# Probabilities times values in two 16-bit parts, two tiles at once, and a new schedule around it

## Time and profile before

| what | value |
|---|---|
| three runs, median (lowest to highest) | 429.23 us (428.6 to 437.26) |
| the profiled execution, its own time | 431.57 us |
| its span, first to last instruction | 429.3 us |
| mean granted TensorE clock | 0.946 of 2.4 GHz |
| busy: PE, DVE, ACT, POOL | 348.2, 302.6, 210.7, 237.0 us |
| scatter-adds L491, 64 of them | 102.9 us busy |
| product L1521, 16 tiles | 35.6 us busy |

### The profile page before, as it was taken

How to read it: one execution, slowest core, us unless ns; L and a number is a source line. 1 busy time by engine, 2 the same in 40 slices (tenths; PEclk the granted TensorE clock), 3 DMA queues, 4 the chain that set the end, 5 groups by cost and what they waited for, 6 DMA issues and landing times.

```text
span 429.3 us, 7070 instructions
## 1 busy us (share of the span) xinstructions
PE 348.2 (81%) x2108; PEld 273.3 (64%) x2108; DVE 302.6 (70%) x953; ACT 210.7 (49%) x540; POOL 237.0 (55%) x219
## 2 busy tenths in 40 slices
PE   0999668778798998669979999987278877987893
PEld 0984336647375877648847788765156766876773
DVE  4599975568646765235777586656679998899875
ACT  3755436252532534353334454432257678676871
POOL 3600085676757668676867788852156545764211
PEclk9999999896978999879998999999869999999999
DMA  8957935575658998766776778557700000000001
GB/s 271 361 176 247 329 99 126 117 178 117 148 99 198 243 279 209 186 134 135 197 171 124 167 164 187 91 61 166 252 2 0 26 1 27 26 24 27 2 25 50
DMA packets 33032, 58.41 MB, mean 136 GB/s; under 512 B 3723, under 2 KB 20451, under 8 KB 32611
## 3 DMA queue, kind: packets, MB, share of 16 engines
q1 hardware_dynamic: 20707, 39.08, 27.9%
q0 software_dynamic: 12288, 18.88, 24.7%
HBM read 40.22 MB, written 17.73 MB: 135 GB/s over the span
## 4 chain that ended last, share of the span: by engine, by line
PE 42%; DVE 27%; issue 11%; ACT 9%; DMA 6%; POOL 4%; DVEq 0%; POOLq 0%; ACTq 0%
PE two L1521 7%; PE two L1541 6%; PE two L1553 5%; DMA acc_d<-W,idxE 4%; PE two L1483 3%; DVE F L1263 3%; PE two L1360 3%; PE two L1409 2%; POOL ny L534 2%; PE two L1435 2%; PE two L1530 2%; PE two L1494 2%; ACT W L789 2%; ACT two L776 2%; DVE WoS L958 2%
## 5 line engine op out<-in xcount | busy, mean ns | idle before, releaser
L491 POOL DMA_INDIRECT acc_d<-W,idxE x64 | 102.9, 1608 | 51.3 <-DVE W L1081 36.0
L472 POOL DMA_INDIRECT W<-tok_d,idxE x56 | 57.6, 1029 | 48.2 <-DVE idxE L1039 31.4
L1117 DVE SCALAR_TENSOR_TENSOR W<-W,two 128x88 f32<-128x88 f32 x64 | 15.6, 244 | 59.9 <-ACT W L703 45.5
L687 ACT ACTIVATE W<-two 128x256 f32<-128x256 f32 x64 | 24.3, 380 | 45.8 <-PE two L1530 40.3
L1521 PE MATMUL two<-A,v 128*128 128x128 f32 x256 | 35.6, 298 | 10.3 <-issue 7.5
L1521 PEld LDWEIGHTS two<-A,v 128*128 128x128 f32 x256 | 34.2, 212 | 13.3 <-issue 12.7
L1667 PE MATMUL two<-W,A 128*128 128x257 f16 x256 | 30.1, 273 | 10.6 <-DVE F L1288 9.9
L1634 PE MATMUL two<-F,wfcT 128*128 128x256 f16 x256 | 32.8, 280 | 4.4 <-DVE A L1256 2.9
L1667 PEld LDWEIGHTS two<-W,A 128*128 128x128 f16 x256 | 23.9, 98 | 16.5 <-DVE F L1288 11.7
L1081 DVE TENSOR_SCALAR W<-two,W 128x256 f32<-128x256 f32 x56 | 26.8, 478 | 8.5 <-PE two L1553 5.1
L776 ACT ACTIVATE two<-two,gwv 128x512 f32<-128x512 f32 x32 | 21.3, 667 | 23.1 <-PE two L1634 23.1
(11 more groups left out here) (237 smaller groups left out, 882.8 us busy)
## 6 DMA issues: line engine op xcount, KB each, us to landing
W<-in_gu SPq DMA_DIRECT2D x20, 352.0 KB
acc_d<-F SPq DMA_DIRECT2D x2, 2176.0 KB, 14.2
F<-in_gu SPq DMA_DIRECT2D x12, 352.0 KB
W<-in_dn SPq DMA_DIRECT2D x20, 176.0 KB
tok_d<-xr SPq DMA_DIRECT2D x2, 1280.0 KB, 5.9
F<-in_dn SPq DMA_DIRECT2D x12, 176.0 KB
x<-in_q SPq DMA_DIRECT2D x4, 512.0 KB, 6.5
A<-in_Wo SPq DMA_DIRECT2D x1, 2048.0 KB, 12.5
```

The source lines that it names most:

```text
L472: pool.indirect_dma_start(out=xg[n % XR], out_offset=None, in_=tok_d[:, :], in_offset=bass.IndirectOffsetOnAxis(ap=idxE[:, n:n + 1], axis=0))\
L491: pool.indirect_dma_start(out=acc_d[n % 2][:, :], out_offset=bass.IndirectOffsetOnAxis(ap=idxE[:, n:n + 1], axis=0), in_=ysb[n % YS], in_o ...
L687: sc.activation(xgT[n % 2], bk_(2)[:, 0:D].rearrange("p (k n) -> p k n", k=KH), ACT.Copy)\
```

## The change

- The values are kept as a high and a low 16-bit part (`v_hi` by ACT, `v_lo` by DVE), and so are the transposed probabilities (`pT_hi`, `pT_lo`); the product is hi*hi + lo*hi + hi*lo.
- Two tiles of one batch share one product of 256 columns (`attend`), 24 instructions of 16 bits for two tiles. `ORDER` now takes two tiles of a batch in turn. ACT copies both results at once, and the projections of both follow in the next pair.
- A half of a transpose is copied by ACT and then subtracted by DVE, and only then may the bank be written again.
- All 16 tiles stand in the loop, from turn 17; behind it stands the last projection alone.
- Tables, slot products and the shared MLP get other turns, ACT takes 8 in place of 10 tiles of the last table pass, and DVE the other 8.
- Ahead of the loop, the transposes of the last two parts of the values follow the first token list, and DVE subtracts four parts; three in place of two of the head sums come behind the first list.

```diff
-START = 19
-LATE = 2
-BESIDE = (NT - LATE) * STEPS
-ACT_T = 10
+START = 17
+BESIDE = NT * STEPS
+ACT_T = 8
...
-DOWN_AT = {1: (0, 0), 2: (0, 1), 6: (1, 0), 7: (1, 1), 11: (2, 0), 12: (2, 1), 16: (3, 0), 17: (3, 1)}
-UP_AT = {3: 1, 8: 2, 13: 3}
-PRODUCT_AT = {4: 1, 9: 2, 14: 3}
+DOWN_AT = {1: (0, 0), 2: (0, 1), 5: (1, 0), 6: (1, 1), 9: (2, 0), 10: (2, 1), 13: (3, 0), 14: (3, 1)}
+UP_AT = {3: 1, 7: 2, 11: 3}
+PRODUCT_AT = {4: 1, 8: 2, 12: 3}
...
-HOT_AT = {2: (1, 0), 3: (1, 1), 4: (1, 2), 7: (2, 0), 8: (2, 1), 9: (2, 2), 12: (3, 0), 13: (3, 1), 14: (3, 2)}
-NUMBER_AT = {2: (1, 0), 3: (1, 1), 7: (2, 0), 8: (2, 1), 12: (3, 0), 13: (3, 1)}
-SLOTS_AT, SPREAD_AT, TURN_AT, TAKE_AT = {5: 1, 10: 2, 15: 3}, {6: 1, 11: 2, 16: 3}, {7: 1, 12: 2, 17: 3}, {8: 1, 13: 2, 18: 3}
+HOT_AT = {2: (1, 0), 3: (1, 1), 4: (1, 2), 7: (2, 0), 8: (2, 1), 9: (2, 2), 13: (3, 0), 14: (3, 1), 15: (3, 2)}
+NUMBER_AT = {2: (1, 0), 3: (1, 1), 7: (2, 0), 8: (2, 1), 13: (3, 0), 14: (3, 1)}
+SLOTS_AT, SPREAD_AT, TURN_AT, TAKE_AT = {6: 1, 12: 2, 17: 3}, {7: 1, 13: 2, 18: 3}, {8: 1, 14: 2, 19: 3}, {9: 1, 15: 2, 20: 3}
...
-ORDER = [p + NP * i for p in range(NP) for i in range(2)]
+ORDER = [NP * b + 2 * p + i for p in range(NP // 2) for b in range(BATCH) for i in range(2)]
+UW = 2 * P
...
 def beside(n):
...
-        v = sb("v", [P, NT, DH])
+        v_hi, v_lo = [sb(n, [P, NT, DH], F16) for n in ("v_hi", "v_lo")]
...
-        probT = [A[:, 2048 + 1024 * i:3072 + 1024 * i].rearrange("p (i j) -> p i j", i=8) for i in range(2)]
+        pT_hi, pT_lo = [A[:, 2048 + 1024 * i:3072 + 1024 * i].bitcast(F16).rearrange("p (i j) -> p i j", i=8) for i in range(2)]
...
-        oT = [F[:, 8128 + 128 * i:8256 + 128 * i] for i in range(2)]
+        oT = [F[:, 8128 + UW * i:8128 + UW * i + UW] for i in range(2)]
...
             def gated(p):
...
-                pool.wait_ge(s0_ready, 2 * p + 2)
+                pool.wait_ge(s0_ready, NT)
...
             def take_v(c):
...
-                sc.activation(v[:, 4 * c:4 * c + 4, :], bk_(c % 2).rearrange("p (t d) -> p t d", t=4), ACT.Copy)\
-                    .then_inc(v_ready, 1)
+                sc.activation(v_hi[:, 4 * c:4 * c + 4, :], bk_(c % 2).rearrange("p (t d) -> p t d", t=4), ACT.Copy)\
+                    .then_inc(v_hi_ready, 1)
...
             def number(g, t0, t1):
...
+            def high_probs(t, h):
+                sc.wait_ge(pT_ps, 2 * t + h + 1)
+                if t >= 2:
+                    sc.wait_ge(o_ps, t // 2)
+                sc.activation(pT_hi[:, 4 * h:4 * h + 4, P * (t % 2):P * (t % 2) + P], bk_(0).rearrange("p (i j) -> p i j", i=4), ACT.Copy)\
+                    .then_inc(pT_hi_ready, 1)
+            def take_oT(u):
+                sc.wait_ge(o_ps, u + 1)
+                if u >= 2:
+                    sc.wait_ge(wo_ps, 2 * u - 2)
+                sc.activation(oT[u % 2], bk_(1)[:, 0:UW], ACT.Copy).then_inc(oT_ready, 1)
             def attention_step(t, step):
...
-                    sc.wait_ge(pT_ps, 2 * t + 1)
-                    if t >= 2:
-                        sc.wait_ge(o_ps, t - 1)
-                    sc.activation(probT[t % 2][:, 0:4, :], bk_(0).rearrange("p (i j) -> p i j", i=4), ACT.Copy)\
-                        .then_inc(pT_act, 1)
-                elif step == 2 and t + 1 < NT:
-                    exps(t + 1)
-                elif step == 3:
-                    sc.wait_ge(o_ps, t + 1)
-                    if t >= 2:
-                        sc.wait_ge(wo_ps, t - 1)
-                    sc.activation(oT[t % 2], bk_(1)[:, 0:P], ACT.Copy).then_inc(oT_ready, 1)
+                    if t % 2 == 0 and t:
+                        take_oT(t // 2 - 1)
+                    high_probs(t, 0)
+                elif step == 2:
+                    high_probs(t, 1)
+                    if t + 1 < NT:
+                        exps(t + 1)
...
             def turn(n):
...
-            for t in range(NT - LATE, NT):
-                for step_ in range(STEPS):
-                    attention_step(t, step_)
+            take_oT(NT // 2 - 1)
...
             def gate(p):
...
+            def low_v(c):
+                ve.wait_ge(v_hi_ready, c + 1)
+                ve.tensor_tensor(v_lo[:, 4 * c:4 * c + 4, :], bk_(c % 2).rearrange("p (t d) -> p t d", t=4),
+                                 v_hi[:, 4 * c:4 * c + 4, :], ALU.subtract).then_inc(v_ready, 1)
...
             def take_projected(t):
-                ve.wait_ge(wo_ps, t + 1)
+                ve.wait_ge(wo_ps, t - t % 2 + 2)
...
-                then(ve.scalar_tensor_tensor(out=s0[:, u, :], in0=bk_(1)[:, 0:D], scalar=rinv[:, t:t + 1], in1=bo_b,
+                then(ve.scalar_tensor_tensor(out=s0[:, u, :], in0=bk_(1)[:, D * (1 - t % 2):D * (1 - t % 2) + D], scalar=rinv[:, t:t + 1], in1=bo_b,
...
+            def low_probs(t, h):
+                ve.wait_ge(pT_hi_ready, 2 * t + h + 1)
+                cols = slice(P * (t % 2), P * (t % 2) + P)
+                ve.tensor_tensor(pT_lo[:, 4 * h:4 * h + 4, cols], bk_(0).rearrange("p (i j) -> p i j", i=4),
+                                 pT_hi[:, 4 * h:4 * h + 4, cols], ALU.subtract).then_inc(pT_lo_ready, 1)
             def attention_step(t, step):
...
-                    if t:
-                        take_projected(t - 1)
-                elif step == 1 and t + 1 < NT:
-                    top(t + 1)
+                    low_probs(t, 0)
+                elif step == 1:
+                    if t + 1 < NT:
+                        top(t + 1)
...
-                    ve.wait_ge(pT_ps, 2 * t + 2)
-                    if t >= 2:
-                        ve.wait_ge(o_ps, t - 1)
-                    ve.tensor_copy(probT[t % 2][:, 4:8, :], bk_(0).rearrange("p (i j) -> p i j", i=4)).then_inc(pT_dve, 1)
+                    low_probs(t, 1)
+                    if t % 2 == 0 and t:
+                        take_projected(t - 2)
...
+                    if t % 2 == 0 and t:
+                        take_projected(t - 1)
...
             def flat_g(a):
...
+            low_v(0)
+            low_v(1)
...
-            head_sum(1)
...
-            head_sum(2)
-            head_sum(3)
+            low_v(2)
+            low_v(3)
+            for i in range(1, 4):
+                head_sum(i)
...
-            for t in range(NT - LATE, NT):
-                for step_ in range(STEPS):
-                    attention_step(t, step_)
+            take_projected(NT - 2)
...
-            turn_v(2)
-            turn_v(3)
...
+            turn_v(2)
+            turn_v(3)
...
             def turn_probs(t, h):
...
-                if h:
-                    pe.wait_ge(pT_act, t + 1)
-                elif t:
-                    pe.wait_ge(pT_dve, t)
+                if t or h:
+                    pe.wait_ge(pT_lo_ready, 2 * t + h)
+                else:
+                    pe.wait_ge(sy_ready, NT // 2)
...
             def project0(t):
-                pe.wait_ge(oT_ready, t + 1)
+                pe.wait_ge(oT_ready, t // 2 + 1)
...
-                pe.matmul(bk_(1)[:, 0:D], oT[t % 2], WoS[:, :], start=True, stop=True).then_inc(wo_ps, 1)
+                pe.matmul(bk_(1)[:, D * (1 - t % 2):D * (1 - t % 2) + D], oT[t // 2 % 2][:, P * (t % 2):P * (t % 2) + P], WoS[:, :],
+                          start=True, stop=True).then_inc(wo_ps, 1)
+            def attend(u):
+                pe.wait_ge(pT_lo_ready, 4 * u + 4)
+                if u:
+                    pe.wait_ge(s0_ready, 2 * u)
+                else:
+                    pe.wait_ge(idxE_ready, NG)
+                for i in range(8):
+                    k = (ORDER[2 * u] // NP) * NP + i
+                    for v, pT in ((v_hi, pT_hi), (v_hi, pT_lo), (v_lo, pT_hi)):
+                        ins = pe.matmul(bk_(1)[:, 0:UW], v[:, k, :], pT[:, i, :], start=(i == 0 and v is v_hi and pT is pT_hi),
+                                        stop=(i == 7 and v is v_lo))
+                ins.then_inc(o_ps, 1)
...
             def attention_step(t, step):
...
-                    if t:
+                elif step == 1:
+                    if t % 2 == 0 and t:
+                        project0(t - 2)
...
-                elif step == 1 and t + 1 < NT:
-                    score(t + 1)
+                    if t + 1 < NT:
+                        score(t + 1)
...
-                elif step == 3:
-                    pe.wait_ge(pT_act, t + 1)
-                    pe.wait_ge(pT_dve, t + 1)
-                    if t:
-                        pe.wait_ge(s0_ready, t)
-                    else:
-                        pe.wait_ge(idxE_ready, NG)
-                    for i in range(8):
-                        ins = pe.matmul(bk_(1)[:, 0:P], v[:, (ORDER[t] // NP) * NP + i, :], probT[t % 2][:, i, :], start=(i == 0),
-                                        stop=(i == 7))
-                    ins.then_inc(o_ps, 1)
+                elif t % 2:
+                    attend(t // 2)
...
             def turn(n):
...
-            for t in range(NT - LATE, NT):
```

(11 more changed lines are left out.)

## The result

The changed kernel takes 435.5 us (median of four runs) where the kernel before took 429.6 in the runs beside it: ratio 1.0148, 95% interval 1.0109 to 1.0186. It is 1.5% slower: clear of the interval, but less than the 2% that counts as a difference. The forecast was 425.2 us; the time lies just above the range's end at 435.0. The profiled execution has 436.2 us of its own and a span of 434.3, 5.0 more than the profiled one of before.

A forecast was written before the change was run, and what follows sets the result against it. PE (2.86 us per expert plus waits) and POOL (3.19 plus waits) were taken as nearly level bounds. +4.4 - 7.6 + 1.9 + 0 + 1.4 - 4.1 = -4.0 us gave a median of 425.2 us, range 418 to 435.

The forecast's parts named there:

- Ahead of the loop, +4.4: Before the first expert: DVE's extra head sum, low-part subtractions and wait for late transposes cost 4.4 us, bounds 3.2 to 5.5.
- Tables, -7.6: In the loop: later slot products spare PE's three 2.60 us waits and half the low clock, 7.6 us gained, bounds 0 to 14.2.
- the fourth rival: Ahead of the first experts: five us of PE work at half speed, +2.5 us, 427.7 us in all; chance 0.08.
- Product, split and two tiles, +1.9 and 0: Loop from turn 17: two more tiles' streaming costs 1.9 us if PE sets the pace; the split's order costs 0.
- My bounds, -6 to +20.8: Limits on the split's cost in the loop: pace falling to 3.27 us, or both halves' extra copy time bare 16 times.
- The sign of being wrong that I named: From expert 19: a pace over 3.5 us per expert with PE waiting for the subtraction; or a first expert not later.
- first rival: In the loop: DVE waits for ACT's high part, PE for DVE; +10.4 us, 435.6 us in all; chance 0.17.
- POOL's floor of 3.19: In the loop while gathers last: POOL unhindered starts a scatter-add, gather included, every 3.19 us, the floor of an expert.
- PE's level: In the loop: PE streams 2.86 us per expert, attention tiles included, plus waits, nearly level with POOL.
- End of the loop, +1.4: Turn 63: both last down products wait for a longer last product and longer copies, 1.4 us, none if POOL is behind.
- Behind the loop, -4.1: After the last scatter-add: without two leftover tiles the first total starts 3.1 to 5.1 us sooner, taken as 4.1.

The follow-up runs named there:

- e5: The kernel before with the later tables, slot products and shared MLP turns alone, old product, two tiles behind the loop: 424.0 us, ratio 0.983.
- e4: The changed kernel with the last pair's product behind PE's last two down products instead of ahead of them: 432.4 us, ratio 1.0086.
- e18: The changed kernel with only ACT's copy `gwv` put ahead of turn 34's steps, which moved nothing, so a repeat: 436.9 us, ratio 1.017.
- e9: The changed kernel, same steps and turns dealt so steps 0 and 1 share a turn, `gwv` copied earlier: 417.5 us, ratio 0.973.
- e10: The changed kernel, same steps and turns dealt so steps 2 and 3 share a turn, `gwv` copied earlier: 445.0 us, ratio 1.038.
- e1: The changed kernel without DVE's subtractions for the low parts of the probabilities, as many products: 427.9 us, ratio 1.0006.
- e2: The kernel before with the changed schedule alone: old product, later tables, all 16 tiles in the loop from turn 18: 435.1 us, ratio 1.015.
- e11: The kernel before with later tables and slot products, old product, steps 0 and 1 sharing a turn in 11 of 14 tiles: 416.8 us, ratio 0.971.
- e13: The kernel before with nothing of the change but steps 0 and 1 sharing a turn in 11 of 14 tiles: 423.2 us, ratio 0.980.
- e14: The changed kernel over the same 47 turns, steps 1 and 2 of every tile sharing a turn: 428.5 us, ratio 0.992.
- e15: The changed kernel over the same 47 turns, step 3 of each tile sharing a turn with step 0 of the next: 424.0 us, ratio 0.981.
- e16: The changed kernel's own deal, but steps 0 and 1 share a turn in the five tiles where 2 and 3 did: 431.8 us, ratio 1.001.
- e17: The changed kernel's own deal, DVE's sums over heads for layer 1 moved from turn 42 to turn 46: 427.6 us, ratio 0.992.

## Why the prediction was wrong

**Ahead of the loop, +4.4: right.** +3.8 at the first tanh (62.96 against 59.18), +3.9 at DVE's first expert, with no cover. The runs with these same instructions ahead of the loop have their first tanh from 62.5 to 65.1, so the agreement is no closer than 1 or 2 us.

**Tables, -7.6: right, its last tenths by luck.** From the first tanh to that of expert 19 it is 67.0 us in place of 74.7, 7.7 less, with 1.9 of loss inside that the sum did not have (below). With the tables alone (e5) it is 68.1, 6.6 less. The three waits of 2.60 are gone, the small ones ahead of `turn_h` that the forecast named are there twice (0.87 and 0.90 us), and the clock came back whole, where I took half: the product of table 1 follows PE's work without idle time (the chain, in order of time), and the clock of the stretch that had 0.50 is 1.00.

```profile
85.59 0.86 PE two L1438 x4
86.45 1.75 PE two L1454 x16
```
```profile
95.00:130.00 35.00, 31.65 (x167) 22.69 (x168) 29.45 (x117) 15.49 (x55) 26.71 (x20) 1.00 0.72 161
```

**The low clock ahead of the first experts** (the fourth rival) came too, inside that sum. Behind DVE's later start PE's clock was 0.73 from 65 to 71 us, where the kernel before had 1.00 from 62 to 67 (in e4 and e18, with the same instructions up to there, it was 0.50 from 65 to 71), and the first expert took longer (the shared product ahead of it, then its up products, beside those of the second expert):

```profile
65.00:71.00 6.00, 4.68 (x18) 3.61 (x19) 0.85 (x5) 2.47 (x7) 0.39 (x1) 0.73 0.16 47
```
```profile
67.28 1.63 PE two L1438 x4
68.92 0.43 PE two L1557 x2
69.34 1.17 PE two L1568 x4
70.52 0.21 PE two L1574
70.73 0.72 PE two L1580 x2
71.45 0.86 PE two L1438 x4
72.31 0.22 PE two L1557 x2
72.53 0.60 PE two L1568 x4
73.13 0.11 PE two L1574
73.24 0.43 PE two L1580 x2
```

So the rule of the Trainium skill that the prediction weighed ("TensorE: Matmul & The Clock Gate", "Part 1: The HAM clock gate": the clock is halved when the array has not been busy of late) held where the forecast took nothing for it. The five pieces take 4.16 us the first time and 2.22 the second, 1.9 us more; in the kernel before only the shared product was longer, 1.13 for 0.86. (The stretch of 303 to 313 that the forecast compares with has PE busy for 0.61 us, not 0.25.)

**Product, split and two tiles, +1.9 and 0: the step that failed.** The loop from expert 19 took 9.6 us more. The failed step is the sentence under the split, "yet PE finds the bank free where the steps fall in different turns. I take 0": it puts the order of the steps at nothing. I had counted how many steps a turn holds on average, 2.3 us for each, and never listed which steps share a turn. What the runs showed in its place: the order alone moves the loop from 141.9 us (e9) to 170.3 (e10), and the changed kernel's own deal stands at 159.2. My bounds, -6 to +20.8, did hold the size (the pace of the lower one, 3.27, is not half of the way from 3.40 to 3.19; that is 3.295, and about -5). The sign of being wrong that I named came: a pace of 3.62, over 3.5, with PE waiting for the subtraction.

The streaming was right where the clock was up: 24 instructions take 2.63 us on the chain (forecast 2.62). Two of the eight took 5.08 and 4.16 us at the lower clock, and the sum had nothing for that.

That the first rival's 435.6 us is nearly the measured 435.5 is luck. Its mechanism, the split on the ring, is a part of the truth: its subtraction is worth 6.9 us here (e1), but hardly shows where the deal keeps the product away from it (e9: 0.5 us of wait with the split in place), and the old product loses more in nearly the same schedule (e2, 13.3 us of loop). Under a good deal for both, the step from e11 to e9 costs the loop 1.4 us (141.9 - 140.5) for two tiles, near the +1.9 of the forecast.

**What the deal explains, and what not.** With steps 0 and 1 together in both, the loop is 141.9 (changed, e9) and 144.1 us (before, e13); with their own deals 159.2 and 149.7. So the deal turns a loss of 9.6 into a gain of 2.2, and even if the copy `gwv` has a few us in it, the deal has most of it: that is shown. Which turns of the changed deal make the 9.6 is not. Steps 2 and 3 share a turn in five tiles (three before), 1 with 2 in four (three), 0 with 1 in four (three), 3 with 0 in four (two). But in the changed kernel only an odd tile's turn of 2 and 3 holds a product, so turns with second transposes and their product are three in either kernel (22, 28 and 63; 31, 47 and 63). Four of the five stand in turns 19 to 28, a stretch in which the changed kernel is faster; the loss comes from expert 33 on. That the 9.6 us are the sum of pair prices is not shown either: the prices from the loops of e10, e14 (rather too high) and e15 over e9 are 1.8, 0.8 and 0.65 us a pair and give 13.0 us for the changed kernel's twelve pairs inside the loop and 7.3 for the seven of before, 3.5 us between the kernels after the 2.2 by which the changed one is better, where 9.6 were measured. e16 shows the same lack of addition: without the five turns of 2 and 3 the loop is only 2.2 us shorter (157.0). e17 shows that DVE's burst in turn 42 has 6 us of the changed loop's 159.2; its share in the kernel before is not known. How late turns and the burst add is open.

**POOL's floor of 3.19 was not reached.** The loops of e11 and e9 come to 3.19 and 3.22 us per expert on average, but their last turns have no gather. From the scatter-add of expert 19 to that of 57 POOL takes 3.34 us per expert in e11, 3.38 in e9, 3.43 in e13, 3.57 before and 3.71 in the changed kernel, and PE is busy for the whole of 250 to 270 us in e11. So both engines still count under a good deal. I read what the kernel before had above the floor as PE's level (2.86 and its waits); a part of it, 3.57 against 3.43, was waits of its deal and of the copy `gwv`.

**End of the loop, +1.4: too small.** It was +3.8. Both kernels hold steps 2 and 3 in turn 63, and the forecast had the longer copy. What it lacked is the clock and a wait. The last product ran from 293.31 to 297.47, 4.16 us in place of the forecast's 2.62, and the clock explains this: its first pairs take 0.61 to 0.64 us, the last ones 0.38. And its transposes stood behind a wait for expert 62 that the kernel before does not have, so they start 2.2 us after the last tanh in place of 0.3:

```profile
290.03 0.31 PE L1574 MATMUL two<-ident,W 128*88 128x128 f32 x1 [0.92 <-DVE W L1140]
```

e9, whose last product has a turn of its own, needs 8.8 us from the last tanh to the last scatter-add against 11.7.

**Behind the loop, -4.1: right.** -4.7, with the load at 304.76 landing 4.2 us later as the last wait.

## What to carry to other kernels

Where side work is dealt over the turns of a pipelined loop by a division, write out which steps share a turn before costing anything: here the same instructions took 417.5 to 445.0 us by that alone, while product, split and two tiles moved 0.7 under a good deal. Keep a producer and its consumer on another engine a turn apart (2 with 3 was the worst, 445.0), and try the pairs that are left: 0 with 1 was the best, and 3 with 0, which need nothing of each other either, took 424.0. Don't add up prices of single turns: it missed twice here (e16, and the 9.6 us). Compute the floor of the slowest queue, and over the turns for which it holds; if the loop is above it, look for waits, and not for streaming time alone.

A better version came out of this: the changed kernel with steps 0 and 1 together, 417.5 us (ratio 0.973), and without product and tiles 416.8 (0.971); both beat both kernels.

## What was not expected of the hardware

A gap on PE can cost twice. Behind the wait of 2.54 us for ACT's copy `gwv` the granted clock of 180 to 190 us is 0.69, and the pair product next to it, which has no wait of its own, takes 5.08 us where another takes 2.63 (the timeline of PE, then the chain):

```profile
184.54 1.22 PE L1580 MATMUL two<-W 88*128 88x256 f32 x2 [2.54 <-ACT gwv L737]
```
```profile
185.76 5.08 PE two L1534 x24
...
236.22 2.63 PE two L1534 x24
```

And the granted clock of 180 to 230 us, the stretch of the long waits, differs with the deal: 0.97 in e9 and 0.87 in e10, 0.90 in the kernel before and 0.88 in the changed one (stretch, length, busy time of PE, PEld, DVE, ACT and POOL, clock, DMA share, GB/s).

```profile
180.00:230.00 50.00, 45.02 (x256) 33.97 (x255) 38.38 (x89) 23.05 (x68) 39.14 (x30) 0.97 0.72 154
```
```profile
180.00:230.00 50.00, 37.41 (x200) 28.29 (x201) 30.28 (x72) 18.41 (x55) 30.91 (x24) 0.87 0.60 135
```
